# Two-layer decoder on one core: fp32 expert weights streamed past stationary tokens in two column tiles, with moved cross keys and a re-laid convolution

## The reference

```
x = x + attention0(ln(x))          # 16 heads, causal
x = x + long_conv(ln(x), k, skip, ctx, ctx)
x = x + moe0(ln(x))                # 2 shared and 16 routed experts, top 4; all experts on all tokens
x = x + attention1(ln(x))          # 16 heads, causal
x = x + cross_attention(ln(x), ctx)  # 32 heads, 8 key and value heads
x = x + moe1(ln(x))                # 32 experts, top 4, 40 slots per expert, and shared ones
```

```
# long_conv: 16 groups of 8 x 8 channel pairs
kv = v[:, :, :, None, :] * x2[:, :, None, :, :]
y  = causal_conv(kv, k) + kv * skip
out = einsum('bhijl,bhil->bhjl', y, x1)
# moe1, per expert e: its (at most 40) tokens Xp[e]
G = Xp @ W_gate ; U = Xp @ W_up          # 40 x 256 times 256 x 128
Y = (silu(G) * U) @ W_down               # 40 x 128 times 128 x 256
out[token of slot] += Y * weight of slot ; out += shared experts
```

## Time and profile before

| | |
|---|---|
| three runs, median (lowest to highest) | 739.84 us (735.91 to 744.57) |
| the profiled execution | 739.16 us, span 737.4 us |
| busy share of the span | PE 86%, PEld 55%, DVE 60%, ACT 32%, POOL 45% |
| mean granted TensorE clock | 0.912 |
| transferred | 47.13 MB, mean 64 GB/s |

### The profile page before, as it was taken

The page is one execution under the profiler, slowest core; times in us unless marked ns, Lnnn a source line. Parts: engine busy times, 40 slices in busy tenths (PEclk is TensorE's granted clock), DMA queues, the critical chain, the costliest instruction groups (busy, mean ns, idle before and its releaser), DMA issues.

```text
span 737.4 us, 14638 instructions
## 1 busy us (share of the span) xinstructions
...
## 2 busy tenths in 40 slices
...
DMA packets 24814, 47.13 MB, mean 64 GB/s; under 512 B 2489, under 2 KB 19147, under 8 KB 23595
## 3 DMA queue, kind: packets, MB, share of 16 engines
...
## 4 chain that ended last, share of the span: by engine, by line
PE 71%; DVE 17%; issue 4%; ACT 4%; DMA 2%; POOL 1%; SPq 1%; DVEq 0%; ACTq 0%; POOLq 0%
PE PS L1053 64%; PE PS L1057 6%; DVE R L865 5%; DVE R L862 3%; DVE stats L710 1%; DMA X<-in_x_dram 1%; DMA R<-qk_scr 1%; DVE X L715 1%; PE PS L1408 1%; DVE R L851 1%; DVE mx L833 1%; DVE wr L1001 1%; ACT xnT L538 1%; DVE xn L725 1%; DVE R L752 1%
## 5 line engine op out<-in xcount | busy, mean ns | idle before, releaser
L1053 PE MATMUL PS<-R 128*128 128x256 f16 (+5 forms) x2260 | 265.0, 282 | 12.3 <-DVE R L862 5.9
L1053 PEld LDWEIGHTS PS<-R 128*128 128x128 f16 (+3 forms) x2260 | 156.0, 103 | 126.5 <-issue 55.0
L833 DVE TENSOR_REDUCE mx<-PS 128x4 bf16<-128x512 f32 x128 | 82.4, 685 | 53.2 <-PE PS L1053 53.2
L601 ACT ACTIVATE R<-PS 128x512 f32<-128x512 f32 x128 | 69.5, 595 | 109.5 <-PE PS L1053 109.5
L426 POOL TENSOR_TENSOR R<-mx,causal 128x512 bf16<-128x512 bf16 x64 | 65.3, 1041 | 76.0 <-DVE mx L833 75.3
L426 POOL TENSOR_TENSOR R<-mx,R 128x512 bf16<-128x512 bf16 x64 | 65.4, 1043 | 32.1 <-DVE mx L833 30.6
L494 POOL TENSOR_TENSOR R<-R 128x256 f16<-128x256 f32 (+1 forms) x50 | 34.1, 683 | 92.9 <-ACT R L631 92.9
L908 DVE TENSOR_TENSOR R<-R,PS 128x512 f32<-128x512 f32 (+1 forms) x50 | 34.3, 686 | 54.6 <-ACT R L644 54.6
L1053 PE MATMUL PS<-xnT,WT 128*128 128x512 f32 (+1 forms) x148 | 55.2, 527 | 2.1 <-ACT xnT L538 2.1
L1053 PE MATMUL PS<-R,wr 128*32 128x128 f32 (+2 forms) x610 | 42.8, 289 | 12.7 <-DVE wr L1001 8.5
L538 ACT ACTIVATE xnT<-PS 128x256 f32<-128x256 f32 x48 | 17.6, 383 | 110.3 <-PE PS L1057 110.1
...
## 6 DMA issues: line engine op xcount, KB each, us to landing
R<-in_experts_dram SPq DMA_DIRECT2D x32, 384.0 KB, 5.2
...
```

Of the source, the lines that this page charges most:

```text
L601: s.activation(PTm[:, u % 4, 4 * k:4 * k + 4, :], bank(2 + (2 * u + k) % 3).rearrange("p (h q) -> p h q", h=4), ACT.Exp, scale=c["sc"]).th ...
L833: v.tensor_reduce(mx[:, t % 4, 4 * k:4 * k + 4], bank(k).rearrange("p (h k) -> p h k", h=4), AX.X, ALU.max).then_inc(S("att_mx"), 1)
L1053: return nc.tensor.matmul(o_, l, r, start=start, stop=stop)
```

## The change

The diff has five parts.

- The keys and values of the cross attention (`cross_keys`) leave the start. They stand behind the scores of the first router, in other banks, and lie in `CT`; the fillers there go from 60 to 24, the 40 in front of the first attention go. SP parks the keys behind the loads of the first expert weights.
- In the convolution the pair axes are (j, i), so that the sum over i reads contiguous elements. The skip input is scaled on ScalarE and multiplied on GpSimd; the skip matmul and the product with `ctx` come after every second group.
- The second expert stage keeps the weights in fp32 and streams them. The tokens are the stationary operand, 64 columns, of which 40 are used; two experts lie in the two 64-wide column tiles. There is no splitting on any engine. The hidden rows are turned (`turn_hidden`) for the down projection, whose result has tokens in its partitions.
- A slot of `EW` is free for its next load once the down projection of its group is done (`y_ps`), where before it was once it was split.
- The result rows, 40 used out of 64, are copied (`Yp`) and packed by 40 small transfers of SP (`PIECES`, `dense_rows`) into `Yd`, from which ScalarE and VectorE scale and split them. The 10 pairs of transposes go.

```diff
-        kx = R1[0:64, 0:1024].bitcast(F16).rearrange("p (s t) -> p s t", s=2)
+        kx = CT[0:64, 0:4, :].rearrange("p b d -> p (b d)").bitcast(F16).rearrange("p (s t) -> p s t", s=2)
...
-        Xp = R2[:, 10240:10240 + 2 * SLOTS].bitcast(F16).rearrange("p (n c s) -> p n c s", n=2, c=DC)
-        yT = R2[:, 12800:12800 + 2 * SLOTS].rearrange("p (c s) -> p c s", c=DC)
+        Xp = R2[:, 10240:10240 + DC * (SLOTS + 24)].rearrange("p (c s) -> p c s", c=DC)
+        Yd = R2[:, 12848:12848 + SC * D].rearrange("p (k d) -> p k d", k=SC)
...
-        esig = xnT[:, 0, 0:640].rearrange("p (n s) -> p n s", n=4)
-        ef = xnT[:, 1, 0:640].rearrange("p (n s) -> p n s", n=4)
-        eh = xnT[:, 0, 640:960].bitcast(F16).rearrange("p (n a s) -> p n a s", n=2, a=2)
...
+        esig = xnT[:, 0, 0:512].rearrange("p (n a i) -> p n a i", n=2, a=2)
+        eh = xnT[:, 0, 512:1024].rearrange("p (n a i) -> p n a i", n=2, a=2)
+        ehT = xnT[:, 1, 0:512].rearrange("p (n a s) -> p n a s", n=2, a=2)
+        Yp = WTs[0][:, :, :, :].rearrange("p a c d -> p (a c d)").rearrange("p (n a d) -> p n a d", n=4, a=2)
...
+        PIECES = [(e, r, 128 * k, min(CAP - r, 128 * (k + 1) - CAP * e - r), k)
+                  for e in range(E1) for k in range(SC) for r in [max(0, 128 * k - CAP * e)]
+                  if r < CAP and 128 * (k + 1) > CAP * e]
         GE = 4
+        def pieces(gr):
+            return 16 * sum(p_[0] // GE == gr for p_ in PIECES)
...
+            def dense_rows(gr):
+                sp.wait_ge(S("yp"), gr + 1)
+                for e, r, first, n, k in PIECES:
+                    if e // GE == gr:
+                        row = CAP * e + r - first
+                        sp.dma_start(Yd[row:row + n, k, :],
+                                     Yp[64 * (e % 2) + r:64 * (e % 2) + r + n, gr % 4, e % GE // 2, :]).then_inc(S(f"yd{gr}"), 16)
...
-                    sp.wait_ge(S("cwA_lo"), (e - WRING) // GE + 1)
-                    sp.wait_ge(S("cwB_lo"), (e - WRING) // GE + 1)
+                    gr = (e - WRING) // GE
+                    sp.wait_ge(S("y_ps"), gr + 1)
                 expert(e)
+                if e >= WRING and e % GE == GE - 1:
+                    dense_rows((e - WRING) // GE)
+            for gr in range((E1 - WRING) // GE, NGR):
+                dense_rows(gr)
...
-                    g.tensor_tensor(kv[:, h % 2, m, :].rearrange("p (b i j) -> p b i j", b=B, i=CI),
-                                    v.unsqueeze(3).broadcast_to([P, B, CI, CI]),
-                                    k.unsqueeze(2).broadcast_to([P, B, CI, CI]),
+                    g.tensor_tensor(kv[:, h % 2, m, :].rearrange("p (b j i) -> p b j i", b=B, j=CI),
+                                    v.unsqueeze(2).broadcast_to([P, B, CI, CI]),
+                                    k.unsqueeze(3).broadcast_to([P, B, CI, CI]),
                                     ALU.mult).then_inc(S("kv_ready"), 1)
+                if h % 2 == 0:
+                    b = h // 2
+                    pool.wait_ge(S("ctx_loaded"), 16)
+                    pool.wait_ge(S("xn_skip"), b + 1)
+                    g.tensor_tensor(ub[:, b, :], ub[:, b, :], CT[:, b, :], ALU.mult).then_inc(S("ub"), 1)
...
             attention(SELF0, 0)
+            for b in range(B):
+                act.wait_ge(S("ln_done"), B + b + 1)
+                s.activation(ub[:, b, :], xn[:, b, :], ACT.Copy, scale=skip[:, 0:1]).then_inc(S("xn_skip"), 1)
...
-            high_parts(0)
-            high_parts(1)
             act.wait_ge(S("gather_ps"), 1)
             for k, (e0, e1) in enumerate(ESPAN):
-                for dc in range(DC):
-                    s.activation(Xp[:, 0, dc, e0 * CAP:e1 * CAP], bank(2 * k + dc, (e1 - e0) * CAP),
-                                 ACT.Copy).then_inc(S("Xp_hi"), 1)
+                s.activation(Xp[:, 0, e0 * CAP:e1 * CAP], bank(2 * k, (e1 - e0) * CAP), ACT.Copy).then_inc(S("Xp0"), 1)
+            def onehots(k):
+                act.wait_ge(S("PmT_ps"), k + 1)
+                s.activation(PmT[:, k, :], PS[:, 6 + k % 2, :].bitcast(F16), ACT.Copy).then_inc(S("PmT"), 1)
             for gr in range(NGR):
                 act.wait_ge(S("eup_ps"), gr + 1)
-                s.activation(esig[:, gr % 4, :], bank(gr % 2, GS), ACT.Silu).then_inc(S("esig"), 1)
-                for k in ([gr] if gr < NGR - 1 else range(gr, SC)):
-                    act.wait_ge(S("PmT_ps"), k + 1)
-                    s.activation(PmT[:, k, :], PS[:, 6 + k % 2, :].bitcast(F16), ACT.Copy).then_inc(S("PmT"), 1)
-                if gr + 2 < NGR:
-                    high_parts(gr + 2)
+                if gr >= 2:
+                    act.wait_ge(S("eh"), gr - 1)
+                s.activation(esig[:, gr % 2], bank(gr % 2).rearrange("p (a w) -> p a w", a=2)[:, :, 0:I1],
+                             ACT.Silu).then_inc(S("esig"), 1)
+                onehots(gr)
+                act.wait_ge(S("ehT_ps"), gr + 1)
+                s.activation(ehT[:, gr % 2], bank(2 + gr % 2, 256).rearrange("p (a s) -> p a s", a=2),
+                             ACT.Copy).then_inc(S("ehT"), 1)
+            for k in range(NGR, SC):
+                onehots(k)
...
-                act.wait_ge(S("Y_ps"), k + 1)
-                s.activation(Y2[:, 0, k, :], bank(4 + k % 4, D), ACT.Copy,
+                for gr in sorted({p_[0] // GE for p_ in PIECES if p_[4] == k}):
+                    act.wait_ge(S(f"yd{gr}"), pieces(gr))
+                s.activation(Y2[:, 0, k, :], Yd[:, k, :], ACT.Copy,
                              scale=wslot[:, k:k + 1]).then_inc(S("y_hi"), 1)
...
             dve.wait_ge(S("ctx_loaded"), 16)
             dve.wait_ge(S("ln_done"), 2 * B)
-            for b in range(B):
-                v.scalar_tensor_tensor(ub[:, b, :], xn[:, b, :], skip[:, 0:1], CT[:, b, :], ALU.mult,
-                                       ALU.mult).then_inc(S("ub"), 1)
-            for b in range(B):
+            def skipped(b):
                 dve.wait_ge(S("skip_ps"), b + 1)
                 v.tensor_tensor(wb[:, b, :], CT[:, b, :], bank(4 + b % 2, 256), ALU.mult).then_inc(S("wb_ready"), 1)
             for h in range(CH):
                 for m in range(DC):
                     i = DC * h + m
                     dve.wait_ge(S("conv_done"), i + 1)
                     x1 = ctxT[:, m, :].rearrange("p (b c) -> p b c", b=B)[:, :, h * CI:(h + 1) * CI]
-                    z = zb[:, i % 4, :].rearrange("p (b i j) -> p b i j", b=B, i=CI)
-                    v.tensor_tensor(z, bank(i % 4).rearrange("p (b i j) -> p b i j", b=B, i=CI),
-                                    x1.unsqueeze(3).broadcast_to([P, B, CI, CI]), ALU.mult).then_inc(S("z"), 1)
+                    z = zb[:, i % 4, :].rearrange("p (b j i) -> p b j i", b=B, j=CI)
+                    v.tensor_tensor(z, bank(i % 4).rearrange("p (b j i) -> p b j i", b=B, j=CI),
+                                    x1.unsqueeze(2).broadcast_to([P, B, CI, CI]), ALU.mult).then_inc(S("z"), 1)
                     dve.wait_ge(S("z"), i + 1)
                     v.tensor_reduce(oT[:, m, :].rearrange("p (b c) -> p b c", b=B)[:, :, h * CI:(h + 1) * CI],
-                                    z.rearrange("p b i j -> p b j i"), AX.X, ALU.add).then_inc(S("oT"), 1)
+                                    z, AX.X, ALU.add).then_inc(S("oT"), 1)
+                    if i % 4 == 3:
+                        skipped(i // 4)
             for b in range(B):
                 dve.wait_ge(S("convT_ps"), b + 1)
...
+            def rows_of(gr):
+                dve.wait_ge(S("y_ps"), gr + 1)
+                if gr >= 4:
+                    dve.wait_ge(S(f"yd{gr - 4}"), pieces(gr - 4))
+                v.tensor_copy(Yp[:, gr % 4], bank(4 + gr % 2).rearrange("p (a d) -> p a d", a=2)).then_inc(S("yp"), 1)
             for gr in range(NGR):
                 dve.wait_ge(S("esig"), gr + 1)
-                link(v.tensor_tensor(ef[:, gr % 4, :], esig[:, gr % 4, :], PS[:, gr % 2, 256:256 + GS], ALU.mult))
-                link(v.tensor_copy(eh[:, gr % 2, 0, :], ef[:, gr % 4, :]))
-                v.tensor_tensor(eh[:, gr % 2, 1, :], ef[:, gr % 4, :], eh[:, gr % 2, 0, :],
-                                ALU.subtract).then_inc(S("eh"), 1)
+                if gr >= 2:
+                    dve.wait_ge(S("ehT_ps"), gr - 1)
+                v.tensor_tensor(eh[:, gr % 2], esig[:, gr % 2],
+                                bank(gr % 2).rearrange("p (a w) -> p a w", a=2)[:, :, I1:2 * I1], ALU.mult).then_inc(S("eh"), 1)
                 if gr >= 1:
-                    k = gr - 1
-                    dve.wait_ge(S("y_ps"), k + 1)
-                    v.tensor_copy(yT[:, :, k * GS:(k + 1) * GS], PS[:, 2 + k % 2, 0:2 * GS].rearrange("p (c s) -> p c s", c=DC)).then_inc(S("yT"), 1)
-                if gr + 2 < NGR:
-                    split_weights(gr + 2)
-            k = NGR - 1
-            dve.wait_ge(S("y_ps"), k + 1)
```

(69 more changed lines are left out.)

95 lines of the change are left out of this document (23 added, 72 removed).

## The result

The changed kernel takes 709.61 us (median of 4 runs, 703.62 to 714.25), the kernel before 740.03 (median of 4): ratio 0.958, 95% interval 0.952 to 0.963. The forecast was 708.0. The profiled execution of the changed kernel is its longest, 714.25 us with a span of 712.5, so the two traces differ by 24.9 us where the medians differ by 30.4.

A forecast was written before the change was run, and what follows sets the result against it. No single engine's busy share was taken as the bound; what TensorE waits for at each place was. Terms -8.5 - 16.9 + 3.4 - 9.6 (and 0) = -31.6 gave span 705.8, forecast 708; range 699 to 726.

The forecast's parts named there:

- Part 1: Start of first attention: without early keys, values and fillers, TensorE starts at 45.2 to 45.5, not 55.13; -8.5 us.
- I take the median, 45.2: First attention's first stack of transfers: last issued about 39.2, landing the median 6.0 us later, at 45.2.
- Part 2: Convolution: contiguous reduction 0.69 instead of 1.08 and skip input off VectorE; two heads take 5.9; -16.9 us.
- with 0.15 for hand-overs: Convolution: VectorE 5.74, TensorE 5.6, GpSimd at most 5.35 per two heads; 0.15 us added for hand-overs gives 5.9.
- Rival A: Convolution: the reduction stays at 1.08, its cost not being the stride; part gives -4.6, total 720.5; 12%.
- Part 3: First router: moved cross keys and values take 8.8 us, then 24 fillers end at 221.6; +3.4 us.
- Part 4: Second experts, up to last down projection: splitting goes, eight groups take 43.6 us instead of 53.2; -9.6 us.
- Rival B: Second expert stage: TensorE's clock stays low, at 0.68; stage +0.4 us, total 718; 22%.
- C: Second expert stage: 64-wide column tiles run one after another; stage +7.8 us, total 726; 6%.
- Nine issues at 0.43: Second expert stage: nine SP issues per group at 0.43 us are 3.9 per period of 5.4, so covered.
- Part 5: Behind the last down projection: rows come by transfers instead of transposes, all ten done at 6.7 us; 0 us.
- D: Second expert stage: SP's queue of 56 issues becomes the bound, kernel slower; 754 at 1.6 us per issue; 4%.

The follow-up runs named there:

- e2: The changed kernel with products in the old order (b, i, j), so the reduction reads with a stride; skip input stays moved: 717.19 us, ratio 0.968.
- e10: The changed kernel with ScalarE copying hidden rows first, GpSimd issuing every second row transfer, and the first router's 24 fillers removed: 696.79 us, ratio 0.942.
- e8: The changed kernel with each row transfer cut into two of half the rows, 80 row issues and 16 loads: 731.44 us, ratio 0.989.

## Why the forecast held, point by point

**Sum.** 708.0 against 709.61, by the right mechanisms; the single terms were off by up to 3.5 us and partly cancel. That the sum comes within 1.6 us is luck as well: the executions of the changed kernel lie 10.6 us apart, and in the trace the untouched stretch gave back 7.6 of 32.5.

**Part 1** (-8.5; -5.0 came). The step "I take the median, 45.2" failed: the last of twelve transfers decides, and it landed 8.4 us behind its issue, so that TensorE started at 48.03; in nine other kernels without the early keys TensorE started at 46.2 to 48.1. The rest is the clock, at 0.50 from the start, where I had allowed 1 us: from the first to the last mask matmul this attention takes 42.6 us, not 40.5.

**Part 2** (-16.9; -19.3). Reduction 0.69 and two heads on TensorE 5.6 as costed; "with 0.15 for hand-overs" was wrong. TensorE had no gaps, and eight pairs took 5.58 each. e2 splits it: stride 12.2, skip input some 7. Rival A is out.

**Part 3** (+3.4; +3.8). The size is right. "They only just bridge the wait for VectorE's gates" was right for the kernel before (0.5 us), but not the use made of it: the moved matmuls alone take 9.3 us where the gates need 7.4 behind the scores, so the 24 fillers bridged nothing. e10 takes them away and gains 2.1.

**Part 4** (-9.6; -12.3). Matmuls, hole and period as costed at clock 1.00 (5.07 forecast, 5.01 measured); the 0.9 for the clock was too low, 3.0 us. Rival B is out (1.00 over the stage, with 0.9 us of transposes in each group), as is C, whatever the tiles do. "Nine issues at 0.43" failed: the loads cost that, the rows 0.74, and I had taken the price from transfers of another shape. I had named a wait for weights in the later groups as what would show me wrong in kind, and there is one, 0.48 us, which makes one group 5.72 us instead of 5.01 (670.40 to 676.12). The Trainium skill (TensorEngine Tiling (Array Packing), Key Properties) says that a change of tiling mode drains the engine; a group's matmuls took 3.64 us (1.82, 0.28, 0.62 and 0.92 by their starts) for the 3.47 costed without it, so 0.17 of the 0.28 that I had put beside it may be that; this is an estimate, and no run takes it apart.

**Part 5** (0; +0.3). ScalarE's ninth scaling waits 0.39 for the rows, the sign that I had named for D, in small.

**Rival D** at 4% had its limit at 0.78 for each of 56 issues, over 43.6 us. They came at 0.69 on average (38.75 us from 646.46), but the stage was shorter too: SP had no pause in it and was as long as the path. The kernel didn't get slower, so D as stated is out, but "nine issues on SP" as a cover held by a hair: 0.48 us of waiting. e8 shows the price beyond, 0.75 for each further issue.
